# Mixture of heads: which of two transposes and copies comes first on TensorE and on ScalarE

## The reference

```python
q = (x @ w_q).reshape(b, n, HEADS, DIM_HEAD).transpose(0, 2, 1, 3)
k = (x @ w_k).reshape(b, n, HEADS, DIM_HEAD).transpose(0, 2, 1, 3)
gates = jax.nn.sigmoid((x @ w_gate).reshape(b, n, HEADS, EXPERTS).transpose(0, 2, 1, 3))
sel = jnp.argmax(gates, axis=-1)
gm = jax.nn.one_hot(sel, EXPERTS, dtype=x.dtype) * gates
values = jnp.einsum('bhne,ehdk,bnd->bhnk', gm, value_experts, x)
sim = jnp.einsum('bhid,bhjd->bhij', q * SCALE, k)
...
attn = jax.nn.softmax(sim, axis=-1)
out = jnp.einsum('bhij,bhjk->bhik', attn, values)
out = jnp.einsum('bhne,ehkd,bhnk->bhnd', gm, output_experts, out)
```

## Time and profile before

| | |
|---|---|
| median of 3 runs | 1832.0 us (1828.65 to 1832.22) |
| the profiled execution | 1838.59 us, of which the span of the trace is 1836.4 us |
| TensorE / VectorE / ScalarE / GpSimd busy | 78% / 66% / 32% / 20% of the span |
| granted clock of TensorE, mean | 0.873 of full |
| the stage of the change | 145 to 698 us of the span |

### The profile page before, as it was taken

The page is one execution under the profiler, slowest core; times in us unless marked ns, Lnnn a source line. Parts: engine busy times, 40 slices in busy tenths (PEclk is TensorE's granted clock), DMA queues, the critical chain, the costliest instruction groups (busy, mean ns, idle before and its releaser), DMA issues. The chain is left out here.

```text
span 1836.4 us, 32252 instructions
## 1 busy us (share of the span) xinstructions
PE 1431.1 (78%) x9741; PEld 1195.3 (65%) x9741; DVE 1202.8 (66%) x3015; ACT 592.9 (32%) x1724; POOL 366.9 (20%) x523
## 2 busy tenths in 40 slices
PE   4767999999999984580623577888789899889998
PEld 2336888888888874470521256666568688778887
DVE  5885667666777764789596857777645366445554
ACT  2331211221221212240210146666523466533232
POOL 4760000000000001100003433444323111122221
PEclk9668999999999996595865569999989899989999
DMA  5541211211211215354526258788512222200000
GB/s 185 178 149 33 58 29 29 57 29 29 57 29 38 49 27 138 102 161 56 126 68 183 88 143 180 177 184 183 119 58 72 68 81 83 60 19 17 23 17 17
DMA packets 194667, 156.14 MB, mean 85 GB/s; under 512 B 18806, under 2 KB 184519, under 8 KB 192296
## 3 DMA queue, kind: packets, MB, share of 16 engines
q1 hardware_dynamic: 163636, 125.26, 27.5%
q10 hardware_dynamic: 30964, 30.08, 5.5%
HBM read 108.47 MB, written 45.76 MB: 84 GB/s over the span
## 5 line engine op out<-in xcount | busy, mean ns | idle before, releaser
L720 DVE TENSOR_TENSOR moa_oe<-moa_mask,moa_ogT 128x1024 fp32r<-128x1024 bf16 x128 | 155.4, 1225 | 36.4 <-PE moa_k_ps L93 33.3
L91 PE MATMUL moa_k_ps<-moa_w_out_hi,moa_oe 128*128 128x256 f32 x512 | 150.4, 294 | 13.6 <-DVE moa_oe L720 13.6
L92 PE MATMUL moa_k_ps<-moa_w_out_lo,moa_oe 128*128 128x256 f32 x512 | 144.1, 282 | 0.0
L93 PE MATMUL moa_k_ps<-moa_w_out_hi,moa_oe 128*128 128x256 f32 x512 | 143.7, 281 | 0.0
L2009 PE MATMUL L_b_ps<-L_v,L_pT 128*128 128x128 f32 x1024 | 131.2, 287 | 1.2 <-issue 1.2
L2009 PEld LDWEIGHTS L_b_ps<-L_v,L_pT 128*128 128x128 f32 x1024 | 124.8, 201 | 6.8 <-issue 6.6
L91 PEld LDWEIGHTS moa_k_ps<-moa_w_out_hi,moa_oe 128*128 128x128 f32 x512 | 97.1, 190 | 22.4 <-issue 16.8
L1666 POOL TENSOR_TENSOR L_att<-L_masked,L_mask_add 128x512 f32<-128x512 f32 x64 | 81.4, 1272 | 151.2 <-DVE L_masked L1738 151.2
L687 DVE COPY_PREDICATED moa_v_sel<-moa_onehot,moa_y_ps 128x512 f32<-128x512 int32 x112 | 82.3, 735 | 35.3 <-DVE moa_v_sel L687 29.7
L1068 PE MATMUL proj_kv_ps<-proj_cT,L_wk 128*128 128x128 f32 x256 | 37.7, 295 | 85.8 <-PEq L1147 64.8
L1999 PE MATMUL L_r_ps<-ident,L_prob 128*128 128x128 f32 x512 | 77.3, 283 | 32.7 <-DVE L_pT L1722 26.1
(11 more groups left out here) (341 smaller groups left out, 3830.5 us busy)
## 6 DMA issues: line engine op xcount, KB each, us to landing
bounce<-L_rel SPq DMA_DIRECT2D x64, 258.0 KB, 4.9
moa_mask<-chosen SPq DMA_DIRECT2D x32, 512.0 KB, 5.9
L_shifted<-bounce SPq DMA_DIRECT2D x64, 256.0 KB, 4.4
L_values<-proj_v ACTq DMA_DIRECT2D x32, 136.0 KB, 2.1
L_v<-L_values SPq DMA_DIRECT2D x32, 136.0 KB, 2.9
ret_staged_values<-in_w_value_dram ACTq DMA_DIRECT2D x8, 512.0 KB, 3.8
ret_staged_outputs<-in_w_out_dram ACTq DMA_DIRECT2D x8, 512.0 KB, 4.0
ret_cT<-in_ctxT_pairs_dram SPq DMA_DIRECT2D x16, 256.0 KB, 2.9
```

What stands on the lines that cost most here:

```text
L91: pe.matmul(out, x_hi, w_hi, start=first, stop=False)
L92: pe.matmul(out, x_hi, w_lo, start=False, stop=False)
L93: return pe.matmul(out, x_lo, w_hi, start=False, stop=last)
L720: dve.tensor_tensor(oe[e % 2][:, :, :, :].rearrange("p a m s -> p a (m s)"), mask[:, e, :, :].rearrange("p m s -> p (m s)").unsqueeze(1).t ...
```

## The change

On TensorE the two transposes of the next batch's input move ahead of the eight transposes of the probabilities. On ScalarE the two copies of the transposed input move ahead of the copy of the probabilities' first half. Every wait moves with its instruction, and none is added or left out.

```diff
@@ ScalarE
-                        act.wait_ge(pT_ps, after(b * 2 + 1))
-                        act.wait_ge(o_done, after(b))
-                        act.activation(probT[:, 0], s_ps[0][:, :, :], ACT.Copy).then_inc(pT_ready, 1)
                     if front:
                         act.wait_ge(xT_ps, after(b + 2))
                         act.wait_ge(y_done, after(b * 8 + 8))
                         act.activation(xnT_hi[:, :, :], t_ps[:, 0:D].rearrange("p (t s) -> p t s", t=DT), ACT.Copy)
                         act.activation(xnT[:, :, :], t_ps[:, 0:D].rearrange("p (t s) -> p t s", t=DT), ACT.Copy).then_inc(xT_ready, 1)
                     if main:
+                        act.wait_ge(pT_ps, after(b * 2 + 1))
+                        act.wait_ge(o_done, after(b))
+                        act.activation(probT[:, 0], s_ps[0][:, :, :], ACT.Copy).then_inc(pT_ready, 1)
                         act.wait_ge(ogT_ps, after(b + 1))
@@ TensorE
+                    if front:
+                        pe.wait_ge(ln.xn_ready, after(b + 2))
+                        pe.wait_ge(ohT_ready, after(b + 1))
+                        for t in range(DT):
+                            last = pe.transpose(t_ps[:, 128 * t:128 * t + 128], ln.xn[:, 128 * t:128 * t + 128], k.ident[:, :])
+                        last.then_inc(xT_ps, 1)
+                    if main:
                         for j in range(2):
                             pe.wait_ge(prob_ready, after(b * 8 + (4 * j + 4)))
                             for m in range(4):
                                 last = pe.transpose(s_ps[j][:, m, :], prob[:, j, m], k.ident[:, :])
                             last.then_inc(pT_ps, 1)
-                    if front:
-                        pe.wait_ge(ln.xn_ready, after(b + 2))
-                        pe.wait_ge(ohT_ready, after(b + 1))
-                        for t in range(DT):
-                            last = pe.transpose(t_ps[:, 128 * t:128 * t + 128], ln.xn[:, 128 * t:128 * t + 128], k.ident[:, :])
-                        last.then_inc(xT_ps, 1)
```

More of the change, by code:

```diff
@@ L791, in step @@
                             last.then_inc(y_done, 1)
[L792 to L796, removed]
                     if front:
@@ L802, in step @@
                         last.then_inc(xT_ps, 1)
+                    if main:
+                        for j in range(2):
+                            pe.wait_ge(prob_ready, after(b * 8 + (4 * j + 4)))
+                            for m in range(4):
+                                last = pe.transpose(s_ps[j][:, m, :], prob[:, j, m], k.ident[:, :])
+                            last.then_inc(pT_ps, 1)
                     if front:
```

## The result

The changed kernel takes 0.9957 of the kernel before, with a 95% interval of 0.9942 to 0.9971 (medians 1822.2 and 1828.8 us, 7 runs each). Beside the second group of experiments it measured 0.9948 (0.9934 to 0.9962). The forecast of 8.25 us out of 1832.0 is a ratio of 0.9955.

A forecast was written before the change was run, and what follows sets the result against it. TensorE's work plus its gaps bound the mixture-of-heads stage, with 12.3 us waited before the router's product. 15 steps x 0.55 us = 8.25 us, from a median of 1832.0 to 1823.8 us; range 1818 to 1828.

The forecast's parts named there:

- The sum: Over the 15 steps that prepare a next batch, `og` starts 0.55 us earlier each: 8.25 us won.
- rival A: VectorE takes up the router logits only when its probabilities copy has ended: 6.30 us won, 1825.7 us; chance 0.14.
- Items 1 and 3: TensorE transposes x first, its wait for `xn` costing nothing; the router's product starts 0.85 to 0.96 us earlier.
- Item 2: ScalarE's copies of x start 0.03 to 0.14 us behind their releaser, done at 370.18 to 370.29 against 371.14.
- Items 4 and 5: Later probabilities transposes and copies cost nothing; the attention product waits for VectorE's half, 0.67 us won, 0.2 to 0.3 idle.
- Item 6: VectorE's logits start 0.60 us behind its probabilities copy's start; `og` follows at 373.62, 0.55 us earlier.
- the sign that I named: At the attention product, a TensorE wait of 0.2 to 0.3 us on VectorE's copy would show the forecast right.
- the two ends that were forecast: Limits on `og`'s start: VectorE's small operations give 373.62, the attention product 373.50 to 373.60; VectorE's is later.
- B: The router product's whole 0.91 us a step comes through: 13.7 us won, 1818.3 us; chance 0.05.
- C: The gap is handed on: the wait before the output experts grows by what is won, 1832.0 us; chance 0.11.
- D: Late `xn` holds TensorE before the probabilities' transposes: half a microsecond beyond the cover costs 7.5 us, 1839.5; chance 0.05.

The follow-up runs named there:

- e1_tensor_order_alone: Kernel before with only TensorE's two groups of transposes exchanged, ScalarE's order left; 1.0002 of the kernel before, period 33.63 us.
- e2_scalar_order_alone: Kernel before with only ScalarE's copies of x put ahead of its copy of the probabilities; 0.9994 of the kernel before, period 33.63 us.
- e3_scalar_copies_both: Changed kernel with VectorE's half of the transposed probabilities also copied by ScalarE; 0.9926 of the kernel before, period 32.85 us.

## Why the prediction was right, point by point

The sum. 0.55 us a step was forecast; `og`, its transposes and the output experts all come 0.55 earlier behind `v`, and the period fell by 0.58 (33.67 to 33.09). The stage, from the first result to the last, fell by 8.5 us. The 0.03 between lies, as it seems, in the profiled execution of the kernel before: its steps but the last took 33.66 to 33.78, and the three experiments that change nothing left 33.63 to 33.64. The runs' ratio, 0.43% or 7.9 us, agrees; its interval (5.3 to 10.6 us) would also hold rival A's 6.30, so it is the rows that decide between the two.

Items 1 and 3. The two transposes of x stand 0.22 ahead of the probabilities, x's copies are done at 367.36, the router's product starts 0.05 behind. It won 0.86 where 0.85 to 0.96 was expected.

Item 2 gave the right end of the copies, but read one of its bounds wrongly. The 0.14 between two copies was called ScalarE's own gap; `e1_tensor_order_alone` shows that the engine overlaps them by 0.11 and that the gap was a wait for TensorE, and `e2_scalar_order_alone` that this wait stays when the copy ahead is taken away. The start behind x's transposes is 0.12 in both kernels (370.36 to 370.48; 366.58 to 366.70), inside the bounds. For the full change the mistake cost nothing; for TensorE's order alone it gave a loss of 3.3 us that does not exist.

Items 4 and 5. Both halves of the probabilities were covered: VectorE's copy starts 0.61 behind `v` as before, ScalarE's ends at 367.84, 0.7 before VectorE's (368.55). The attention product starts 0.06 behind that end, 0.21 later than TensorE's order allows (367.41 + 0.49 + 0.50 = 368.40), as the last step had shown. Only the sign that I named was wrong: this idle time is not in the view of waits, because the products ahead drain until 368.56 and the engine counts as busy.

Item 6. The logits start 0.60 behind the copy's start, 0.08 before its reported end; rival A is out. For this pair of operations the trace also goes against the sentence of the Trainium skill, VectorE: DVE Perf Modes, "The DRAIN you can't avoid", that the prediction cites. The prediction left out how the Trainium skill goes on in that section: "A next op that is not held starts earlier"; the 0.60 agrees with that, and what would hold an operation was not varied here. `og` starts 0.05 behind `scale_o` (370.65) and 2.09 behind the attention product: the two ends that were forecast 0.02 to 0.12 apart coincide. That is why more work on VectorE costs (0.48 of 0.54). Less work on it should then help only with an earlier attention product; `e3_scalar_copies_both` has both at once, and no run takes them apart.

The other rivals. B would have needed an earlier `v`: it didn't move. C: the wait at the output experts is unchanged, 13.6 us. D: `xn` was early enough, and the transposes follow the value products as before (366.20 behind a product that starts at 365.97, the step of 0.23 of the products among themselves).

The whole execution. The profiled ones differ by 16.4 us in span, twice the gain; 8.4 of that lie before the stage's last result. What lies behind it took 1141.6 and 1133.6 us here, and 1123.8 to 1134.5 in the eight experiments, all with the same code there. What in it varies was not followed up. So single executions cannot be compared for an effect of this size, only ratios against the kernel before on the same chip, or the stage's own rows.

## What to carry to other kernels

A stall behind two queues goes only when it is taken out of both: here either exchange alone gave nothing, and both together 0.55 us of the 0.82 that the waits showed. Before counting a wait as gain, follow the engines that would be late next; the last step, which lacks the moved work, showed the new limit beforehand. And the slack of an engine changes with the order: a memset that is free in one order costs nearly its length in the other, and moving a copy to ScalarE gains 0.24 us a step in the one and loses 0.25 in the other, so work is to be dealt out again after each such change.

## What the runs showed of the hardware

ScalarE starts a copy some 0.1 us before the one ahead has ended (269.92 against 269.43 + 0.60), if nothing is waited for. VectorE did the same between `v`, its copy and the logits (0.08 us before the reported end), but not ahead of the memset, which began 0.06 behind the copy's reported end (269.17 + 0.68 to 269.91); why these differ is open. The copy `xnT_hi`, whose two waits have a sequencer instruction between them in the loop, starts there 0.11 to 0.12 us behind its releaser; in the first and the last of its 16 runs, outside the loop, it starts 0.03 to 0.04 behind it. That the sequencer instruction is the reason was not tested by itself.
